# A graph network of three passes over 400000 edges: 25 ranks per register load, and edge features and place rows in one transfer per five steps

## The reference

```python
# pass 0
all_feat = concat([x[dst], x[src], edge_attr, u_per_node[dst]])
agg = segment_sum(relu(all_feat @ W1 + b1), dst, 12500)
x = layernorm(x + relu(concat([x, agg, u_per_node]) @ W2 + b2))
# passes 1 and 2, with W, We and a batch norm of their own
h = x @ W + b
agg = segment_sum(h[src] + edge_attr @ We + be, dst, 12500) + h
h = batchnorm(relu(agg) + bias)
# at the end: layernorm(x + h)
```

## Time and profile before

| | us |
|---|---|
| median of 3 runs | 15650.02 (15645.94 to 15651.08) |
| the profiled execution, its own time | 15667.31 |
| its span, first to last instruction | 15665.6 |
| PE busy | 6858.2 |
| DVE busy | 4970.4 |
| POOL busy | 9376.9 |

### The profile page before, as it was taken

The page is one execution under the profiler, slowest core; times in us unless marked ns, Lnnn a source line. Parts: engine busy times, 40 slices in busy tenths (PEclk is TensorE's granted clock), DMA queues, the critical chain, the costliest instruction groups (busy, mean ns, idle before and its releaser), DMA issues.

```text
span 15665.6 us, 128029 instructions
## 1 busy us (share of the span) xinstructions
PE 6858.2 (44%) x29865; PEld 5870.1 (37%) x29865; DVE 4970.4 (32%) x12980; ACT 396.2 (3%) x790; POOL 9376.9 (60%) x9927
## 2 busy tenths in 40 slices
PE   3555665666666565333333333334333333333333
PEld 3455555555555555222222222223222222222222
DVE  1333333333333333233233323233332233233223
ACT  0000000000000000000000000000000000000000
POOL 5555555555555554666666666665666666666664
PEclk9666666556565655555555555555555555555555
DMA  2233333333333332111111212112111111111111
GB/s 57 65 67 67 68 68 67 67 68 68 67 69 67 67 69 47 34 34 34 34 34 34 34 34 35 34 34 46 24 23 23 23 23 23 23 23 23 23 23 33
DMA packets 1678916, 688.51 MB, mean 44 GB/s; under 512 B 1375841, under 2 KB 1518977, under 8 KB 1678734
## 3 DMA queue, kind: packets, MB, share of 16 engines
q1 hardware_dynamic: 1363181, 359.16, 11.0%
q0 software_dynamic: 315680, 328.70, 10.9%
HBM read 658.74 MB, written 28.14 MB: 44 GB/s over the span
## 4 chain that ended last, share of the span: by engine, by line
another core or an unknown queue 47%; DVE 18%; DVEq 14%; issue 11%; PE 8%; POOL 1%; DMA 0%; SPq 0%; ACT 0%; ACTq 0%; POOLq 0%
DVE by_rank L940 13%; DVEq L909 11%; PE sum_ps L653 4%; DVE hit L925 3%; PE pre_ps L630 1%; PE pre_ps L627 1%; DVEq L933 1%; DVEq L930 1%; DVEq L925 1%; DVEq L931 1%; POOL ranked L528 1%; DVE summed_in L919 1%; DVE scratch L913 0%; DVEq L335 0%
## 5 line engine op out<-in xcount | busy, mean ns | idle before, releaser
L546 POOL DMA_INDIRECT rows<-source_table,index x6250 | 5927.0, 948 | 4120.7 <-issue 2000.2
L940 DVE TENSOR_TENSOR by_rank<-by_rank,sum_ps 64x128 f32 (+1 forms) x9375 | 2626.0, 280 | 7858.2 <-remote 6978.5
L653 PE MATMUL sum_ps<-hit,message 128*64 128x128 f32 (+1 forms) x12500 | 2844.0, 404 | 3493.7 <-DVE hit L925 1462.8
L546 POOL DMA_INDIRECT message<-source_table,index x3125 | 2955.6, 946 | 1639.9 <-issue 888.1
L653 PEld LDWEIGHTS sum_ps<-hit,message 128*64 128x64 f32 (+1 forms) x12500 | 2375.0, 237 | 3845.3 <-issue 3780.9
L653 PE MATMUL sum_ps<-hit,rows 128*64 128x128 f32 x6250 | 1428.3, 412 | 3091.1 <-DVE hit L925 2056.6
L653 PEld LDWEIGHTS sum_ps<-hit,rows 128*64 128x64 f32 x6250 | 1205.0, 218 | 3314.1 <-issue 3307.4
L925 DVE TENSOR_TENSOR hit<-out_ps,edge_place 128x640 f32<-128x640 f32 x1875 | 1539.6, 821 | 1349.2 <-issue 1201.9
L627 PE MATMUL pre_ps<-w_edge,scratch 96*128 96x192 f32 x2500 | 983.0, 487 | 1356.3 <-DVE summed_in L919 867.9
L630 PE MATMUL pre_ps<-scratch 128*128 128x64 f32 x6250 | 1331.5, 360 | 462.0 <-issue 461.8
L630 PEld LDWEIGHTS pre_ps<-scratch 128*128 128x128 f32 x6250 | 1298.6, 280 | 538.9 <-issue 511.5
(11 more groups left out here) (156 smaller groups left out, 1413.5 us busy)
## 6 DMA issues: line engine op xcount, KB each, us to landing
rows<-source_table,index POOLq DMA_INDIRECT x6250
scratch<-ranked SPq DMA_DIRECT2D x3125, 32.0 KB
scratch<-place_rows SPq DMA_DIRECT2D x625, 160.0 KB
scratch<-in_edge_t_steps SPq DMA_DIRECT2D x625, 96.0 KB
message<-in_edge_steps SPq DMA_DIRECT2D x625, 80.0 KB
message<-source_table,index POOLq DMA_INDIRECT x3125
xt<-in_x_t SPq DMA_DIRECT2D x28, 224.0 KB
index<-in_src_steps SPq DMA_DIRECT2D x375, 12.5 KB
```

Of the source, the lines that this page charges most:

```text
L546: nc.gpsimd.indirect_dma_start(to, None, source_table[l][:, :], bass.IndirectOffsetOnAxis(ap=index[:, at.j, s:s + 1], axis=0))\
L653: one = mm(tile_sum(at.half, s)[0:w, :], (message if l < 2 else rows)[:, at.slot, s, 0:w], hit[:, at.half, s, :], start=True, stop=True)
L940: V.tensor_tensor(at_rank[s], at_rank[s], tile_sum(at.half, s)[0:w, :], ALU.add)\
```

## The change

SP and VectorE have 25 rank registers instead of five and load them once per group of five steps, at slot 0. The edge features and place rows of pass 0 get two halves of five steps each (`t`), and one transfer fills a half, with a semaphore of its own for each. The waits of these transfers and of the register load on SP are for the group five steps back and stand before the wait of the windows. The place rows move from `scratch` into `edge_cat`, whose constants VectorE now writes after the steps of pass 0. PE and VectorE wait for the joined transfers at slot 0 alone.

```diff
-        eat = part(RING * 2 * P, STACK * C).rearrange("p (u n e) -> p u n e", u=RING, n=2)
+        eat = part(TURNS * RING * 2 * P, STACK * C).rearrange("p (t u n e) -> p t u n e", t=TURNS, u=RING, n=2)
-        place_row = part(RING * S * P // 2).bitcast(bf16).rearrange("p (u n) -> p u n", u=RING)
+        place_row = edge_cat.rearrange("p b w -> p (b w)")[:, 0:TURNS * RING * S * P // 2].bitcast(bf16)\
+            .rearrange("p (t u n) -> p t u n", t=TURNS, u=RING)
...
-            rank_regs = [ctx.enter_context(sp.register(f"rank{s}")) for s in range(S)]
+            rank_regs = [ctx.enter_context(sp.register(f"rank{s}")) for s in range(RING * S)]
...
                     m = at + 6
+                    if l == 0 and m.real and m.slot == 0:
+                        t = m.j // RING
+                        wait(sp, pre_done, m.number - RING)
+                        sp.dma_start(eat[:, t, :, :, :], a["edge_t_steps"][bass.ds(m.number, RING), :, :, :]
+                                     .rearrange("k c n e -> c k n e")).then_inc(eat_in[t], 16)
+                        wait(sp, spread_made, m.number - RING)
+                        sp.dma_start(place_row[:, t, :, :], place_rows[bass.ds(m.number * S, RING * S), :]
+                                     .rearrange("(k s) e -> k (s e)", k=RING).partition_broadcast(P))\
+                            .then_inc(place_row_in[t], 16)
+                        sp.reg_load(rank_regs, tile_bytes[:, bass.ds(m.number * S, RING * S)])
                     if l == 0 and m.real:
+                        at_byte = [sp.snap(r, min_val=0, max_val=NPAD * ROW)
+                                   for r in rank_regs[m.slot * S:(m.slot + 1) * S]]
                         wait(sp, pre_done, m.number - RING + 1)
-                        sp.reg_load(rank_regs, tile_bytes[:, bass.ds(m.number * S, S)])
-                        at_byte = [sp.snap(r, min_val=0, max_val=NPAD * ROW) for r in rank_regs]
                         for s in range(S):
                             sp.dma_start(window_bytes[:, m.slot, s, :], ranked_bytes[:, bass.ds(at_byte[s], P * ROW)]
                                          .rearrange("o (p w) -> (o p) w", p=P)).then_inc(window_in[m.slot], 16)
-                        wait(sp, spread_made, m.number - RING + 1)
-                        sp.dma_start(place_row[:, m.slot, :], place_rows[bass.ds(m.number * S, S), :]
-                                     .rearrange("s e -> (s e)").partition_broadcast(P))\
-                            .then_inc(place_row_in[m.slot], 16)
-                        sp.dma_start(eat[:, m.slot, :, :],
-                                     a["edge_t_steps"][bass.ds(m.number, 1), :, :, :]
-                                     .rearrange("k c n e -> (k c) n e")).then_inc(window_in[m.slot], 16)
...
-                pe.wait_ge(window_in[m.slot], m.turn * (16 * (S + 1)) + 16 * (S + 1))
+                pe.wait_ge(window_in[m.slot], m.turn * (16 * S) + 16 * S)
+                if m.slot == 0:
+                    pe.wait_ge(eat_in[m.j // RING], m.index_loads(0))
...
-                    if at.real:
-                        dve.reg_load(add_regs, tile_ranks[:, bass.ds(at.number * S, S)])
+                    if at.real and at.slot == 0:
+                        dve.reg_load(add_regs, tile_ranks[:, bass.ds(at.number * S, RING * S)])
                     if l == 0 and o.real:
-                        dve.wait_ge(place_row_in[o.slot], o.loads())
+                        if o.slot == 0:
+                            dve.wait_ge(place_row_in[o.j // RING], o.index_loads(0))
...
                 if l == 0:
+                    V.memset(edge_cat[:, :, C + 1:C + 2], 1.0)
+                    V.tensor_copy(edge_cat[:, :, C:C + 1], degree[:, :].unsqueeze(2))
                     dve.wait_ge(xn_in, 16)
```

More of the change, by code:

```diff
@@ L127, in part @@
             return scratch[0:parts, at - n:at]
-        eat = part(RING * 2 * P, STACK * C).rearrange("p (u n e) -> p u n e", u=RING, n=2)
+        eat = part(TURNS * RING * 2 * P, STACK * C).rearrange("p (t u n e) -> p t u n e", t=TURNS, u=RING, n=2)
         window = part(RING * S * F).rearrange("p (u s w) -> p u s w", u=RING, s=S)
         window_bytes = window.bitcast(mybir.dt.uint8)
-        place_row = part(RING * S * P // 2).bitcast(bf16).rearrange("p (u n) -> p u n", u=RING)
+        place_row = edge_cat.rearrange("p b w -> p (b w)")[:, 0:TURNS * RING * S * P // 2].bitcast(bf16)\
+            .rearrange("p (t u n) -> p t u n", t=TURNS, u=RING)
         spread = part(2 * S * P).rearrange("p (u s e) -> p u s e", u=2, s=S)
-        assert at <= NB * F and NB * F + TILES <= SCRATCH
+        assert at <= NB * F and NB * F + TILES <= SCRATCH and TURNS * RING * S * P // 2 <= NB * (C + 2)
         hit = sb("hit", [P, 2, S, P])
@@ L215, in build @@
         window_in = [sem(f"window_in_{u}") for u in slot]
-        place_row_in = [sem(f"place_row_in_{u}") for u in slot]
+        place_row_in = [sem(f"place_row_in_{t}") for t in range(TURNS)]
+        eat_in = [sem(f"eat_in_{t}") for t in range(TURNS)]
         spread_made = sem("spread_made")
@@ L620, in before_relu @@
                 pe.compute_val(m.number + 1)
-                pe.compute_val(m.turn * (16 * (S + 1)) + 16 * (S + 1))
+                pe.compute_val(m.turn * (16 * S) + 16 * S)
                 wait(pe, added, m.number - 1)
                 pe.wait_ge(spread_made, m.number + 1)
-                pe.wait_ge(window_in[m.slot], m.turn * (16 * (S + 1)) + 16 * (S + 1))
+                pe.wait_ge(window_in[m.slot], m.turn * (16 * S) + 16 * S)
+                if m.slot == 0:
+                    pe.wait_ge(eat_in[m.j // RING], m.index_loads(0))
                 for q in range(0, S, STACK):
                     n = min(STACK, S - q)
-                    mm(pre_ps[:, m.half, q * F:(q + n) * F], eat[0:n * C, m.slot, q // STACK, :],
+                    mm(pre_ps[:, m.half, q * F:(q + n) * F], eat[0:n * C, m.j // RING, m.slot, q // STACK, :],
                        w_edge[0:n * C, 0:n * F], start=True, stop=False)
@@ L819, in _ @@
             V.memset(first[:, NB:NB + 1], float(E))
-            V.memset(edge_cat[:, :, C + 1:C + 2], 1.0)
             V.memset(glob_b[G:G + 1, :], 1.0)
@@ L874, in _ @@
             V.tensor_scalar(some[:, :], degree[:, :], 1.0, None, ALU.min).then_inc(some_known, 1)
-            V.tensor_copy(edge_cat[:, :, C:C + 1], degree[:, :].unsqueeze(2))
             dve.wait_ge(rank_ps, 1)
@@ L894, in _ @@
                 V.tensor_copy(by_tile[:, c, :], turn_ps[:, c % 2, 0:ROWS]).then_inc(places_kept, 1)
-            add_regs = [ctx.enter_context(dve.register(f"add_rank{s}")) for s in range(S)]
+            add_regs = [ctx.enter_context(dve.register(f"add_rank{s}")) for s in range(RING * S)]
             for l in range(3):
@@ L907, in steps @@
                     o, m = at + 3, at + 1
-                    if at.real:
-                        dve.reg_load(add_regs, tile_ranks[:, bass.ds(at.number * S, S)])
+                    if at.real and at.slot == 0:
+                        dve.reg_load(add_regs, tile_ranks[:, bass.ds(at.number * S, RING * S)])
                     if l == 0 and o.real:
-                        dve.wait_ge(place_row_in[o.slot], o.loads())
+                        if o.slot == 0:
+                            dve.wait_ge(place_row_in[o.j // RING], o.index_loads(0))
                         wait(dve, pre_done, o.number - 1)
-                        V.tensor_scalar(spread[:, o.half, :, :].rearrange("p s e -> p (s e)"), place_row[:, o.slot, :],
+                        V.tensor_scalar(spread[:, o.half, :, :].rearrange("p s e -> p (s e)"), place_row[:, o.j // RING, o.slot, :],
                                         lane[:, 0:1], None, ALU.is_equal).then_inc(spread_made, 1)
@@ L930, in steps @@
                             dve.compute_val(at.number * S + s)
-                        at_rank = [by_rank[0:w, bass.ds(dve.snap(r, min_val=0, max_val=NPAD), P)] for r in add_regs]
+                        at_rank = [by_rank[0:w, bass.ds(dve.snap(r, min_val=0, max_val=NPAD), P)] for r in add_regs[at.slot * S:(at.slot + 1) * S]]
                         for to in at_rank:
```

## The result

The changed kernel takes 15429.33 us (median of four runs, 15406.50 to 15444.65) beside 15647.98 of the kernel before on the same chip: ratio 0.9866, 95% interval 0.9853 to 0.9879. It is 219 us faster. The forecast was 440; the measured time lies inside the range, and the forecast is twice the gain.

What follows compares the result with a forecast made beforehand. POOL's gathers and gaps were taken as the bound, with SP's full queue delaying the index in pass 0. Saving 3.5 us in each of 125 groups, 440 us, gave 15667 - 440 = 15227, less 17: 15210 us; range 14800 to 15730.

Steps and rivals of the forecast that it cites:

- What bounds the kernel: All passes: POOL's gathers, 6.25 us a step, plus gaps; in pass 0 SP's full queue makes the index late.
- SP's saving: SP in pass 0: 43.8 us a group shrinks by 18 to 27%, to 32 to 36; SP then waits.
- The register load: SP and VectorE, slot 0: a load of 25 costs 4 to 5 us, so loading per group stays as it is.
- The index gap: POOL in pass 0, waiting for the next group's index: taken as gone, 5.0 us a group.
- The other gap: POOL in pass 0, waiting for `added`: 8.1 us stays, once every four to five steps.
- Rival D: POOL in pass 0: the gap only moves from the index to `added`; within 30 us of 15650; chance 0.08.
- Rival C: POOL in pass 0: half the index gap stays, the long load standing before it; 15400 to 15500 us; chance 0.14.
- pass 1's pace: Rival B: SP's relief brings pass 0 to 7.28 us a step, 919 us less, 14730; chance 0.12.
- Passes 1 and 2: Passes without windows: zero change, since their gap follows POOL's gathering and not VectorE; within 30 us.
- The transfers' burst: Pass 0: joined transfers move the same bytes ahead of slot 0's windows; hidden, without cover up to 9 us a group.

Runs made afterwards that it cites:

- i1: The kernel before with only the wide register loads (25 ranks once a group on SP and VectorE), transfers per step: 15624.26 us, ratio 0.9974.
- f1: The changed kernel with five ranks per register load again, so the joined transfers alone: 15453.76 us, ratio 0.9872.
- g2: The changed kernel with one window transfer a step in pass 0 instead of five: 15161.97 us, ratio 0.9830.
- f2: The changed kernel, in pass 0 the index loaded ahead of its group's other loads and waiting for `added` instead of `tile_summed`: 15352.04 us, ratio 0.9803.
- g1: The changed kernel with four gathers a step instead of five, in all passes: 12853.63 us, ratio 0.8334.
- i2: The changed kernel with the product of spread and window made for two of five tiles in pass 0: 15309.17 us, ratio 0.9773.
- e3: The kernel before, in pass 0 the index loaded ahead of its group's other loads and waiting for `added` instead of `tile_summed`: 12681.21 us, ratio 1.0001.
- f3_both: The changed kernel with the early index and each group's ranks starting at a multiple of 16 bytes: 15404.23 us, ratio 0.9839.
- g3_paced: The changed kernel with four empty instructions behind every gather of POOL: 15280.42 us, ratio 0.9904.

## Why the prediction was half right

- **What bounds the kernel.** That POOL's gathers and gaps make up each step was right. That SP's full queue was what made pass 0 dear was wrong: i1 freed it and gained 0.26%.
- **SP's saving.** Forecast: 18 to 27% less time, and SP becomes an engine that waits. It waits 2060 us of 5234. Right in kind, too small in size: what is left beside its waits is 25.4 us a group for 42.9, 41% less. A count of instructions does not give it: i1 leaves out 4% of them, and 18% of this time goes.
- **The register load.** I took 4 to 5 us; measured 5.08 on SP and 5.59 on VectorE for three of four groups, 1.6 to 1.9 for the fourth. The rule of the Trainium skill, "Runtime: NRT & Kernel Launch", section "Instruction fetch mechanics", some 200 ns per register even in bulk, agrees with this trace for starts off 16 bytes: 5.08 / 25 = 0.203 us on SP, 0.224 on VectorE. The page has these loads from HBM (section "Terms"), those of this kernel come from SBUF. For starts at a multiple of 16 bytes it does not, 1.84 / 25 = 0.074, and the measurement decides.
- **The index gap, the step that failed.** "I take the index gap as gone: 5.0 us a group." It was not: 584 of 686 us stayed, 4.7 us a group for 5.5. The step assumed that the index came late by SP's full queue. SP has time now and the gap stands all the same, with long loads (584 us), with short ones (f1, 567) and with four fifths of the windows gone (g2, 434). What SP stands for there is the index load's own wait for `tile_summed`, which neither the section on the kernel before nor the prediction names. And where the gap was taken away (f2), its 550 us were worth 80, since POOL then stood for `added`.
- **The other gap, the term that was mis-sized.** I let 8.1 us stay once every four to five steps and had 39.35 to 41.4 us a group; it is 41.9. The 8.1 were read off two gaps; the mean of the pass was 7.1, and it fell to 5.9. So more of the gain came from the gap that I had staying (149 us) than from the one that I had going (102); that the time still fell into the range is partly luck. A gap is not a thing that stays while another goes. In passes 1 and 2 the gaps fit a long-run price of 1.44 us a gather (g1). In pass 0 something comes on top, and a gap that is closed reopens there for the most part, though not wholly, under another name. Rival D had this mechanism at a chance of 0.08. Rival C has the size, but not its reason: the gap did not shrink by half, and the long load does not keep it (f1). For pass 1's pace, 7.28 us a step, rows of before had the price already: 5 x 1.25 and 1.0 of gaps in both passes without windows, whatever they waited for.
- **Passes 1 and 2.** Forecast zero; -3 and +8 us. Right, as was the reason: their gap does not follow VectorE, whose idle before its additions covers the long load.
- **The transfers' burst.** Hidden, as forecast: PE's waits for transfers in pass 0 come to 6.8 us. The joined transfers bring about 1.3 of the 1.4% (f1). Whether that comes from SP's missing instructions or from the fewer and longer packets is not separated.

Open is why a step of pass 0 costs 1.1 us more than one of pass 1 where there is hold-back. Windows explain at most 0.19 us of it (g2), three of five products 0.21 (i2); the rest wasn't found. Open too is what the early index is worth in the kernel before, since e3 ran only where nothing is gained, and how much of the index gap is its place in SP's queue and how much its wait. And open is what holds instructions back on three of the experiments' chips and not on two; the traces show each gather of POOL alike on all.

The best version is f2_after_early: 15352.04 us, 0.9803 of the kernel before and 0.5% under the changed one, on a chip with hold-back. On one without, every version that ran took 12671 to 12690 us, with the kernel before at 12678 and 12680.

## What to carry to other kernels

A queue with no waits looks like a bound; free it in a cheap experiment before summing what its relief must bring, and price the gaps of the engine behind it together and not one by one. When several causes take turns in ending the same engine's idle time, closing one of them gives back little. An edit that moves a load and changes its wait tests two things; look first at what the load itself waits for. And run the kernel before beside every version: here the dearer chip took 23% longer, and the change under study was worth 1.4% or nothing.

## What the runs showed of the hardware

- The same program takes 12678 or 15656 us by the chip it runs on. On the dearer chips instructions of SP that take 0.029 us elsewhere take up to 1.4 while POOL gathers. In the kernel before, of 282 address instructions issued 20 us or more after POOL's last gap of over 2 us had begun, and outside any gap, 219 took over 0.5 us; of 805 issued within a gap, 4 us or more after its start, none did. In passes 1 and 2 a gather costs 1.44 us in the long run there instead of 1.25.
- A register load from SBUF costs 5.59 us for 25 registers on VectorE, and 1.84 if its first word lies at a multiple of 16 bytes (all loads in f3_both, one in four in the changed kernel); on SP it is 5.08 and 1.65. For five registers the two levels are 1.18 and 0.59. From five to 25 that is 0.22 us a register off the boundary and 0.06 on it.
- Four empty instructions behind a gather of POOL left its pace as it was: the next gather came 0.30 us after the last as before (g3_paced).
